# Moving one group of transposes into the second up unit, and the result stores to GpSimd's queue, in a graph-and-experts layer

## The chip, the cores and the metric

One core of a Trainium2 chip runs the whole layer. The metric is device time in microseconds (us). Three runs of the kernel before gave 1040.35, 1040.83 and 1041.01 us, median 1040.83.

## The reference, cut to what matters

A layer norm, two graph layers beside a linear attention, then a second layer norm and a mixture of experts over 625 rows of 1024 features. The change lies in the experts alone (8 routed experts, each row goes to 2; D = F = 1024):

```python
h = jax.nn.silu(jnp.einsum('nd,edf->nef', xf, w1))
ye = jnp.einsum('nef,efd->ned', h, w2)
routed = jnp.einsum('ne,ned->nd', combine, ye)
shared = jax.nn.sigmoid(xf @ shared_gate_w) * (jax.nn.silu(gate) * up @ shared_down)
return (routed + shared).reshape(b, t, d)
```

## The kernel before, in words

Every float32 product is made of three passes over a high and a low part of each operand (`passes`, L1985 to L1990). ScalarE (ACT) casts the high part, VectorE (DVE) subtracts it to get the low part. Weights stream from HBM in jobs of half a matrix, each in four pieces of 512 KB; `split_hi` (L789) and `split_lo` (L1186) split a piece, on ACT and DVE.

The expert stage works in blocks: seven fixed ones (q = 0 to 6, `expert`), each with rows of one expert, then a loop over dynamic blocks, which runs once on these inputs. Block q has one row tile or two (`ROWS_OF`, L55). Here q = 1 and q = 6 have one tile of 128 rows (`ONE`, L161); q = 0, 2, 3, 4, 5 have two and are "turned" (`TURNED`, L162): their second product comes out by features and is transposed back (`rows_back`, L2406); the loop's block has two and is not turned.

In a one-tile block TensorE (PE) computes the two up units ("hu", q, 0) and ("hu", q, 1), each 8 x 3 matmuls over half of the 1024 hidden features (`hidden_tokens`, L2422). ACT puts their silu into he_t (L1107). PE transposes each half of he_t with four 128 x 128 transposes (`hidden_across`, L2433, through `transposes`, L2030 to L2035). ACT casts the result (he high, L1117, through L805), DVE subtracts (he low, L1862, through L1205), and the down units ("y", q, h, s) read both (L2508). PE's order in such a block is: first up unit, the last transposes of the turned block before it (`rest_of`), second up unit, transposes of he_t's first half, 8 transposes of the next block's first rows (xg, `rows_across`), transposes of he_t's second half, down units. PE waits for he low by `arrivals` (L2459): first half before k = 0 of the first down unit, second half before k = 4.

Results go from PSUM to one of two staging rows y_s by ACT (`out_rows`, L1074). ACT waits for an earlier store of that row (`y_stored`), copies (L1083), frees the PSUM slot, and issues the store to expert_rows in HBM from its own queue (L1091).

GpSimd (POOL) fetches the next block's rows: `gather_rows(q + 1)` (L738; one indirect DMA for each row tile) as soon as DVE has done the low parts of block q's rows (`rows_in[q]`), so that xg is free. For the dynamic blocks `gather_block` (L746) first copies two index columns, drains, then issues two indirect DMAs. PE waits for them (`xg_loaded`, L2500). After the loop POOL waits for all stores (L772), then gathers each token's two expert rows (L777); DVE adds them up (L1938) and SP and ACT store the output.

PSUM is a ring of four slots in an order written out by hand (`units`, `between`, L168). Queues are in order. The DMA queues in the profile: q1 is SP's, q10 ACT's, q0 POOL's.

Of the kernel before, what the change touches and what calls it, by code (L numbers as in the profile page):

```python
# [5 lines left out]
def gps_layer(nc, x, src, dst, w_self0, w_neigh0, b0, w_self1, w_neigh1, b1,  # L6
# [31 lines left out]
    HW = D // 2  # L38
    HK = KF // 2
# [9 lines left out]
    BC = len(BROWS)  # L49
    CAPS = (208, 208, 152, 152, 152, 128, 128)  # L50
    ORDER = (3, 7, 1, 4, 2, 5, 6)
    FIXED = len(ORDER)
    assert sorted(ORDER) == list(range(1, X)) and len(CAPS) == FIXED and max(CAPS) <= B
    CAP = [CAPS[r - 1] for r in ORDER]
    ROWS_OF = [(128, c - 128) if c > 128 else (c,) for c in CAP] + [BROWS]  # L55
# [128 lines left out]
    LOOP = FIXED  # L184
# [55 lines left out]
    with ctx:  # L240
# [270 lines left out]
        lo_out = sem("lo_out")  # L511
# [156 lines left out]
        def _(pool):  # L668
# [69 lines left out]
            def gather_rows(q):  # L738

                for s, rows in enumerate(ROWS_OF[q]):  # L740
                    t = TILE_AT[q] + s
                    nc.gpsimd.indirect_dma_start(
                        out=xg[0:rows, s, :], out_offset=None, in_=xn2_d,
                        in_offset=bass.IndirectOffsetOnAxis(ap=cols_f[0:rows, t:t + 1], axis=0)).then_inc(xg_loaded, 16)

            def gather_block(at_block):  # L746

                for s in range(BC):
                    nc.gpsimd.tensor_copy(idx2[0:BROWS[s], s:s + 1], cols[0:BROWS[s], s, at_block])
                nc.gpsimd.drain()  # L750
                for s in range(BC):
                    nc.gpsimd.indirect_dma_start(
                        out=xg[0:BROWS[s], s, :], out_offset=None, in_=xn2_d,
                        in_offset=bass.IndirectOffsetOnAxis(ap=idx2[0:BROWS[s], s:s + 1], axis=0)).then_inc(xg_loaded, 16)

            gather_rows(0)
            for q in range(1, FIXED):
                pool.wait_ge(lo_out, rows_in[q - 1])
                gather_rows(q)
            pool.wait_ge(table_ready, 1)  # L760
            blocks = pool.value_load(table[0:1, 1, 0:1], min_val=1, max_val=MAXB - 1)
            pool.wait_ge(lo_out, rows_in[FIXED - 1])
            gather_block(slice(0, 1))
            with pool.Fori(0, blocks) as j:

                pool.wait_ge(lo_out, j * BR + R0)
                gather_block(bass.ds(j + 1, 1))

            pool.wait_ge(xg_loaded, blocks * (16 * BC) + gathered[LOOP])
            pool.wait_ge(lo_out, blocks * BR + R0)  # L770
# [12 lines left out]
        def _(act):  # L783
            copy = nc.scalar.copy

            def wait_unit(key, base=None):
                act.wait_ge(ready[slot(key)], use(key) + 1 if base is None else base * BU + (use(key) + 1))

            def split_hi(job, base=None, quarters=(0, 1), pieces=range(PARTS)):  # L789

                b = job % 2
                if job >= 2:
                    wait_unit(last_unit[job - 2], base)
                if job >= J_X:
                    for s in pieces:
                        act.wait_ge(part_loaded[(job - J_X) % 2][s], by(16 * ((job - J_X) // 2 + 1), base, 32))
                        copy(w_hi[b][:, s * PK:(s + 1) * PK, :], raw_part(job, s)).then_inc(hi_done, 1)  # L797
                    return
                for s in quarters:
                    act.wait_ge(w_loaded[s], 16 * (job + 1))  # L800
                    copy(w_hi[b][:, s * HK:(s + 1) * HK, :], w_raw[s][:, :, :]).then_inc(hi_done, 1)  # L801
# [272 lines left out]
            def out_rows(q, h, s, j=None):  # L1074

                key, tiles, rows = ("y", q, h, s), len(ROWS_OF[q]), ROWS_OF[q][s]
                wait_unit(key, j)

                b = row_buffer(q, h, s)
                before = stores[q][b] + (0 if ONE[q] else 16 * h)  # L1080
                if before:
                    act.wait_ge(y_stored[b], by(before, j, 32))
                copy(y_s[0:rows, b, :], PS(key)[0:rows, 0, :]).then_inc(y_copied, 1)  # L1083
                act.wait_ge(y_copied, by(copies[q] + h * tiles + s + 1, j, 2 * BC))
                act.sem_inc(free[slot(key)], 1)
                if j is None:
                    r = FIRST_ROW[q] + s * 128
                    to = y_d[r:r + rows, h * HW:(h + 1) * HW]
                else:
                    to = y_block(j, s, h * HW, (h + 1) * HW)  # L1090
                act.dma_start(to, y_s[0:rows, b, :]).then_inc(y_stored[b], 16)  # L1091

            def rest_of(q):

# [4 lines left out]
            def hidden_tokens(q):  # L1099

                job, rows = J_X + 4 * q, ROWS_OF[q][0]
                for h in range(2):
                    key = ("hu", q, h)
                    if h == 0:
                        split_hi(job + 1)
                    wait_unit(key)
                    nc.scalar.activation(he_t[0:rows, h, :], PS(key)[0:rows, 0, :], ACT.Silu).then_inc(silu_done, 1)  # L1107
                    act.wait_ge(silu_done, silus[q] + h + 1)
                    act.sem_inc(free[slot(key)], 1)
                    if h == 0:  # L1110
                        split_hi(job + 2)
                        rest_of(q - 1)

            def hidden_across(q, h):

                key, rows = ("ht", q, h), ROWS_OF[q][0]
                hi_of(key, he_hi[:, h * HK:(h + 1) * HK, 0:rows], PB(key)[:, 0:HK * rows].rearrange("p (k t) -> p k t", t=rows))  # L1117
# [28 lines left out]
            def expert(q, j=None):  # L1146

                job = J_X + 4 * q
                if ONE[q]:
                    hidden_tokens(q)  # L1150
                    hidden_across(q, 0)
                else:
                    hidden_features(q, j)
                for key in xe_units(q + 1)[:2]:
                    rows_hi(key, j)
                if ONE[q]:
                    hidden_across(q, 1)
                if TURNED[q]:
                    turned_out(q)
                    return  # L1160
                for h in range(2):
                    split_hi(job + 3 + h, j, pieces=range(PARTS) if h or ONE[q] else range(1, PARTS))
                    for s, rows in enumerate(ROWS_OF[q]):
                        out_rows(q, h, s, j)
                        if h == s == 0:
                            for later in xe_units(q + 1)[2:]:
                                rows_hi(later, j)
# [807 lines left out]
        def _(pe):  # L1975
# [21 lines left out]
            def weights_in(job, k, base=None):  # L1997

                if k % PK == 0:
                    pe.wait_ge(lo_done, by(count_at(job, k // PK), base, 4 * PARTS))  # L2000
# [421 lines left out]
            def hidden_tokens(q):  # L2422

                job, rows = J_X + 4 * q, ROWS_OF[q][0]
                for h in range(2):
                    key = ("hu", q, h)
                    claim(key)
                    by_tokens(key, PS(key)[0:rows, 0, :], (xe_hi, xe_lo), job + h, slice(0, rows),
                              comes=lambda k: weights_in(job + h, k)).then_inc(ready[slot(key)], 1)
                    if h == 0:  # L2430
                        rest_of(q - 1)

# [58 lines left out]
            def expert(q, j=None):  # L2491

                job = J_X + 4 * q
                pe.wait_ge(lo_out, by(rows_in[q], j, BR))
                if ONE[q]:
                    hidden_tokens(q)
                    hidden_across(q, 0)
                else:
                    hidden_features(q, j)
                pe.wait_ge(xg_loaded, by(gathered[q + 1], j, 16 * BC))  # L2500
                for key in xe_units(q + 1)[:2]:
                    rows_across(key, j)
                if TURNED[q]:
                    turned_out(q)
                    return
                if ONE[q]:
                    hidden_across(q, 1)
                for h in range(2):  # L2508
                    for s, rows in enumerate(ROWS_OF[q]):
                        key = ("y", q, h, s)  # L2510
                        claim(key, j)
                        by_tokens(key, PS(key)[0:rows, 0, :], HE, job + 2 + h, slice(s * 128, s * 128 + rows),
                                  arrives=arrivals(q, j) if h == s == 0 else None,
                                  comes=(lambda k: weights_in(job + 2 + h, k, j)) if s == 0 else None).then_inc(ready[slot(key)], 1)
                        if h == s == 0:
                            for later in xe_units(q + 1)[2:]:
                                rows_across(later, j)
# [43 lines left out]
```

## Time and profile before

| what | value |
|---|---|
| median of three runs | 1040.83 us |
| the profiled execution's own time | 1040.68 us |
| its span, first to last instruction | 1038.9 us |
| PE busy in the span | 1022.6 us (98%) |
| DVE, ACT, POOL busy | 63%, 44%, 8% |
| granted TensorE clock, mean | 0.999 of full speed |
| chain that ended last, by engine | PE 86%, DVE 4%, ACT 4%, DMA 2% |
| DMA queues' share of 16 engines' span | q1 35.7%, q0 5.4%, q10 2.1% |

The span plus 1.8 us is the execution's time. Expert blocks fill the stretch from about 704 to 1007 us; after 1007 us come the gathers of the results and the last products. A row of a timeline has the start in us, the duration in us, engine, line, operation, output and inputs, and in brackets the engine's idle time before it with what ended it. In a chain of waits each row is start, duration, and what the end of the kernel waited for at that time.

### The profile page before, as it was taken

The page shows a single profiled execution, that of the slowest core. Times are in us where ns is not written, and L with a number is a line of the kernel's source. Part 1 is how long each engine was busy: PE and PEld are TensorE (multiplying, and loading weights), DVE is VectorE, ACT ScalarE, POOL GpSimd, SP SyncE. Part 2 cuts the span into 40 slices and gives each one's busy share as a digit, 9 for nine tenths or more (in the row PEclk, how much of TensorE's full clock was granted, in tenths as well). Part 3 has the DMA queues.
Part 4 walks back from the last instruction along what each step waited for, and adds up shares of the span by engine and source line. Part 5 has one row for each costly group of instructions (what it writes and reads, how often), then busy time and mean ns, then how long its engine had stood idle before and what let it go on. Part 6 is the DMA issues. An engine that isn't in the chain of part 4 may idle for free.

```text
span 1038.9 us, 16292 instructions
## 1 busy us (share of the span) xinstructions
PE 1022.6 (98%) x6224; PEld 914.7 (88%) x6224; DVE 658.4 (63%) x970; ACT 460.2 (44%) x731; POOL 79.2 (8%) x123
## 2 busy tenths in 40 slices
PE   7999999999999999999999999999999999999998
PEld 5889998787888899987878899998989999998977
DVE  6789968666655765234337365124878787787846
ACT  4423344557777622221122342212666575567630
POOL 6000010000000000000000007000101000010103
PEclk9999999999999999999999999999999999999999
DMA  9821112033212221262200524233789677688918
GB/s 354 313 82 51 73 41 82 7 113 125 82 61 82 82 81 35 106 222 81 81 1 1 180 83 110 87 117 139 253 303 353 236 264 266 229 269 301 343 39 298
DMA packets 76694, 156.44 MB, mean 151 GB/s; under 512 B 8489, under 2 KB 8987, under 8 KB 76618
## 3 DMA queue, kind: packets, MB, share of 16 engines
q1 hardware_dynamic: 65656, 127.30, 35.7%
q0 software_dynamic: 6416, 20.00, 5.4%
q10 hardware_dynamic: 4546, 8.10, 2.1%
q8 instruction: 49, 0.80, 0.3%
q14 instruction: 27, 0.22, 0.1%
HBM read 133.89 MB, written 21.49 MB: 150 GB/s over the span
## 4 chain that ended last, share of the span: by engine, by line
PE 86%; DVE 4%; ACT 4%; DMA 2%; DVEq 2%; issue 1%; POOL 1%; ACTq 0%; POOLq 0%; SPq 0%
PE ps L1988 19%; PE ps L1990 19%; PE ps L1989 19%; PE ps L2452 7%; PE ps L2477 6%; PE ps L2453 3%; PE ps L2478 2%; PE ps L2087 1%; PE ps L2319 1%; PE ps L2250 1%; PE ps L2320 1%; PE ps L2251 1%; PE ps L2101 1%; PE ps L2034 1%; DMA y_second<-expert_rows,slots 1%
## 5 line engine op out<-in xcount | busy, mean ns | idle before, releaser
L1199 DVE TENSOR_TENSOR w_lo<-w_raw,w_hi 128x2048 fp32r<-128x2048 f32 x41 | 93.1, 2288 | 38.8 <-ACT w_hi L801 36.7
L2452 PE MATMUL ps<-xe,w_hi 128*128 128x304 f32 (+2 forms) x384 | 107.3, 357 | 0.0
L1988 PE MATMUL ps<-w_hi,xt_hi 128*128 128x512 f32 (+1 forms) x240 | 96.0, 400 | 3.5 <-DVEq L1509 2.0
L801 ACT CAST w_hi<-w_raw 128x2048 fp32r<-128x2048 f32 x41 | 77.1, 1908 | 45.2 <-PE ps L2320 36.2
L2453 PE MATMUL ps<-xe,w_lo 128*128 128x152 f32 (+2 forms) x384 | 94.4, 246 | 0.0
L1990 PE MATMUL ps<-w_hi,xt_lo 128*128 128x512 f32 (+1 forms) x240 | 93.6, 390 | 0.0
L1989 PE MATMUL ps<-w_lo,xt_hi 128*128 128x512 f32 (+1 forms) x240 | 93.6, 390 | 0.0
L1193 DVE TENSOR_TENSOR w_lo<-w_raw,w_hi 128x1024 fp32r<-128x1024 f32 x68 | 79.8, 1221 | 13.7 <-ACT w_hi L797 11.7
L2477 PE MATMUL ps<-he,w_hi 128*128 128x304 f32 (+1 forms) x320 | 88.2, 355 | 0.0
L797 ACT CAST w_hi<-w_late 128x1024 fp32r<-128x1024 f32 x64 | 63.0, 1053 | 45.0 <-PE ps L1990 18.4
L1193 DVE TENSOR_TENSOR w_lo<-w_late,w_hi 128x1024 fp32r<-128x1024 f32 x64 | 75.2, 1221 | 7.5 <-ACT w_hi L797 4.8
L797 ACT CAST w_hi<-w_raw 128x1024 fp32r<-128x1024 f32 x68 | 66.9, 1051 | 28.2 <-PE ps L2478 18.8
L1988 PE MATMUL ps<-xt_hi,w_hi 128*128 128x314 f32 x256 | 79.4, 310 | 0.0
L1989 PE MATMUL ps<-t_lo,w_hi 128*128 128x314 f32 x256 | 78.8, 308 | 0.0
L1988 PE MATMUL ps<-t_hi,w_hi 128*128 128x314 f32 x256 | 78.8, 308 | 0.0
L1990 PE MATMUL ps<-xt_hi,w_lo 128*128 128x314 f32 x256 | 78.7, 307 | 0.0
L1990 PE MATMUL ps<-t_hi,w_lo 128*128 128x314 f32 x256 | 78.7, 307 | 0.0
L1989 PE MATMUL ps<-xt_lo,w_hi 128*128 128x314 f32 x256 | 78.6, 307 | 0.0
L2478 PE MATMUL ps<-he,w_lo 128*128 128x152 f32 (+1 forms) x320 | 77.6, 242 | 0.0
L2453 PEld LDWEIGHTS ps<-xe,w_lo 128*128 128x128 f32 x384 | 73.3, 191 | 0.1
L2452 PEld LDWEIGHTS ps<-xe,w_hi 128*128 128x128 f32 x384 | 72.1, 188 | 1.3
L915 ACT ACTIVATE src_oh<-iota_c,src_f 128x128 f16<-128x128 bf16 x196 | 62.3, 389 | 19.6 <-DVE o_s L1576 15.0
(371 smaller groups left out, 2355.0 us busy)
## 6 DMA issues: line engine op xcount, KB each, us to landing
w_raw<-in_L_ffn_w SPq DMA_DIRECT2D x64, 512.0 KB, 5.7
w_late<-in_L_ffn_w SPq DMA_DIRECT2D x64, 512.0 KB, 5.1
w_raw<-in_L_gnn_W_neigh SPq DMA_DIRECT2D x8, 1024.0 KB, 6.0
w_raw<-in_L_gnn_W_self SPq DMA_DIRECT2D x8, 1024.0 KB, 5.1
w_raw<-in_L_ffn_shared_gate_up SPq DMA_DIRECT2D x8, 1024.0 KB, 6.0
expert_rows<-ctx_s POOLq DMA_DIRECT2D x15, 512.0 KB, 13.4
w_raw<-in_L_mix_Wv SPq DMA_DIRECT2D x4, 1024.0 KB, 14.8
w_raw<-in_L_mix_Wk SPq DMA_DIRECT2D x4, 1024.0 KB, 5.7
```

What stands on the lines that cost most here:

```text
L797: copy(w_hi[b][:, s * PK:(s + 1) * PK, :], raw_part(job, s)).then_inc(hi_done, 1)
L801: copy(w_hi[b][:, s * HK:(s + 1) * HK, :], w_raw[s][:, :, :]).then_inc(hi_done, 1)
L915: nc.scalar.activation(src_oh[b][:, c, :], iota_c[:, 0:128, 0], ACT.Abs, bias=src_f[:, g * GC + c:g * GC + c + 1]).then_inc(src_abs, 1)
L1193: V_.tensor_tensor(w_lo[b][:, k, :], raw_part(job, s), as32(w_hi[b][:, k, :]), ALU.subtract).then_inc(lo_done, 1)
L1199: V_.tensor_tensor(w_lo[b][:, k, :], w_raw[s][:, :, :], as32(w_hi[b][:, k, :]), ALU.subtract).then_inc(lo_done, 1)
L1988: mat(out_ap, lh, rh, start=start, stop=False)
L1989: mat(out_ap, lh, rl, start=False, stop=False)
L1990: return mat(out_ap, ll, rh, start=False, stop=stop)
L2452: mat(PS(key)[:, a, 0:2 * width], wh[:, k, w_cols], xe[:, :, k, 0:width], start=k == 0, stop=False)
L2453: last = mat(PS(key)[:, a, 0:width], wl[:, k, w_cols], xe_hi[:, k, 0:width], start=False, stop=k == KF - 1)
L2477: mat(PS(key)[:, a, 0:2 * width], wh[:, k, w_cols], he[:, :, k, 0:width], start=k == 0, stop=False)
L2478: last = mat(PS(key)[:, a, 0:width], wl[:, k, w_cols], he_hi[:, k, 0:width], start=False, stop=k == KF - 1)
```

## The change

Two edits. (1) In one-tile blocks the transposes of he_t's first half are called inside the second up unit, before its k = 4 (half of its 24 matmuls are issued then); ACT casts their result before the second half's silu; PE's and ACT's calls after the unit go away. (2) The stores of result rows leave ACT's program and are issued by POOL, each behind a wait for its copy (y_copied). In POOL's order the stores of block q - 1's second half (if turned) and of block q's first half (both halves, if q is not turned) stand behind the gather of block q + 1's rows; in the loop the four stores stand behind the gather.

```diff
--- before.py
+++ after.py
@@ -753,18 +753,39 @@
                         out=xg[0:BROWS[s], s, :], out_offset=None, in_=xn2_d,
                         in_offset=bass.IndirectOffsetOnAxis(ap=idx2[0:BROWS[s], s:s + 1], axis=0)).then_inc(xg_loaded, 16)
 
+            def store_rows(q, h, s, j=None):
+
+                rows, b = ROWS_OF[q][s], row_buffer(q, h, s)
+                pool.wait_ge(y_copied, by(copies[q] + h * len(ROWS_OF[q]) + s + 1, j, 2 * BC))
+                if j is None:
+                    r = FIRST_ROW[q] + s * 128
+                    to = y_d[r:r + rows, h * HW:(h + 1) * HW]
+                else:
+                    to = y_block(j, s, h * HW, (h + 1) * HW)
+                pool.dma_start(to, y_s[0:rows, b, :]).then_inc(y_stored[b], 16)
+
             gather_rows(0)
-            for q in range(1, FIXED):
-                pool.wait_ge(lo_out, rows_in[q - 1])
-                gather_rows(q)
             pool.wait_ge(table_ready, 1)
             blocks = pool.value_load(table[0:1, 1, 0:1], min_val=1, max_val=MAXB - 1)
-            pool.wait_ge(lo_out, rows_in[FIXED - 1])
-            gather_block(slice(0, 1))
+            for q in range(FIXED):
+                pool.wait_ge(lo_out, rows_in[q])
+                if q + 1 < FIXED:
+                    gather_rows(q + 1)
+                else:
+                    gather_block(slice(0, 1))
+                if q and TURNED[q - 1]:
+                    store_rows(q - 1, 1, 0)
+                    store_rows(q - 1, 1, 1)
+                for h in range(1 if TURNED[q] else 2):
+                    for s in range(len(ROWS_OF[q])):
+                        store_rows(q, h, s)
             with pool.Fori(0, blocks) as j:
 
                 pool.wait_ge(lo_out, j * BR + R0)
                 gather_block(bass.ds(j + 1, 1))
+                for h in range(2):
+                    for s in range(BC):
+                        store_rows(LOOP, h, s, j)
 
             pool.wait_ge(xg_loaded, blocks * (16 * BC) + gathered[LOOP])
             pool.wait_ge(lo_out, blocks * BR + R0)
@@ -1083,12 +1104,6 @@
                 copy(y_s[0:rows, b, :], PS(key)[0:rows, 0, :]).then_inc(y_copied, 1)
                 act.wait_ge(y_copied, by(copies[q] + h * tiles + s + 1, j, 2 * BC))
                 act.sem_inc(free[slot(key)], 1)
-                if j is None:
-                    r = FIRST_ROW[q] + s * 128
-                    to = y_d[r:r + rows, h * HW:(h + 1) * HW]
-                else:
-                    to = y_block(j, s, h * HW, (h + 1) * HW)
-                act.dma_start(to, y_s[0:rows, b, :]).then_inc(y_stored[b], 16)
 
             def rest_of(q):
 
@@ -1103,6 +1118,8 @@
                     key = ("hu", q, h)
                     if h == 0:
                         split_hi(job + 1)
+                    else:
+                        hidden_across(q, 0)
                     wait_unit(key)
                     nc.scalar.activation(he_t[0:rows, h, :], PS(key)[0:rows, 0, :], ACT.Silu).then_inc(silu_done, 1)
                     act.wait_ge(silu_done, silus[q] + h + 1)
@@ -1148,7 +1165,6 @@
                 job = J_X + 4 * q
                 if ONE[q]:
                     hidden_tokens(q)
-                    hidden_across(q, 0)
                 else:
                     hidden_features(q, j)
                 for key in xe_units(q + 1)[:2]:
@@ -2422,11 +2438,18 @@
             def hidden_tokens(q):
 
                 job, rows = J_X + 4 * q, ROWS_OF[q][0]
+
+                def arrive(h, k):
+
+                    weights_in(job + h, k)
+                    if h == 1 and k == HK:
+                        hidden_across(q, 0)
+
                 for h in range(2):
                     key = ("hu", q, h)
                     claim(key)
                     by_tokens(key, PS(key)[0:rows, 0, :], (xe_hi, xe_lo), job + h, slice(0, rows),
-                              comes=lambda k: weights_in(job + h, k)).then_inc(ready[slot(key)], 1)
+                              comes=lambda k: arrive(h, k)).then_inc(ready[slot(key)], 1)
                     if h == 0:
                         rest_of(q - 1)
 
@@ -2494,7 +2517,6 @@
                 pe.wait_ge(lo_out, by(rows_in[q], j, BR))
                 if ONE[q]:
                     hidden_tokens(q)
-                    hidden_across(q, 0)
                 else:
                     hidden_features(q, j)
                 pe.wait_ge(xg_loaded, by(gathered[q + 1], j, 16 * BC))
```

## Rows read from the trace of the kernel before

**Rows 1.** PE's waits from 700 to 1039 us: total, times, longest.

```profile
PE ps L1988 <- DVEq L1207: 1.8, 3, 0.7
```

**Rows 2.** Timeline of PE, block 1, around he_t's transposes.

```profile
770.25 0.60 PE L2034 MATMUL ps<-ident,he_t 128*128 128x128 f32 x4
770.69 1.04 PE L2034 MATMUL ps<-ident,xg 128*128 128x128 f32 x8
771.61 0.63 PE L2034 MATMUL ps<-ident,he_t 128*128 128x128 f32 x4
772.95 0.50 PE L1988 MATMUL ps<-w_hi,he 128*128 128x512 f32 x1 [0.71 <-DVEq L1207]
```

**Rows 3.** Chain of waits, block 1, from 769 to 773 us.

```profile
769.78 0.59 ACT y_s L1083
...
770.82 0.61 ACT he_t L1107
...
772.15 0.70 DVE he L1205
```

**Rows 4.** Timeline of PE, block 6: the same wait.

```profile
951.47 0.50 PE L1988 MATMUL ps<-w_hi,he 128*128 128x512 f32 x1 [0.71 <-DVEq L1207]
```

**Rows 5.** Timeline of PE, block 1: first matmuls behind a group of transposes.

```profile
764.67 0.47 PE L1988 MATMUL ps<-w_hi,xe 128*128 128x512 f32 x1
764.99 0.39 PE L1989 MATMUL ps<-w_lo,xe 128*128 128x512 f32 x1
765.22 0.40 PE L1990 MATMUL ps<-w_hi,xe 128*128 128x512 f32 x1
```

**Rows 6.** Timeline of DVE, block 1: weights split, and he low's second half.

```profile
765.93 4.63 DVE L1193 TENSOR_TENSOR w_lo<-w_raw,w_hi 128x1024 fp32r<-128x1024 f32 x4 [1.66 <-ACT w_hi L797]
...
774.66 0.69 DVE L1205 TENSOR_TENSOR he<-ps,he 128x512 fp32r<-128x512 f32 x1
```

**Rows 7.** Lines L1091 and L731: DMA issues by ACT and POOL (ns), and L731's landing.

```profile
L1091 ACTq DMA_DIRECT2D expert_rows<-y_s x28: 314/339/396, 754.8 to 1007.8; - x28
...
L731 POOL DMA_DIRECT2D cols_f<-token_of_slot x12: 532/563/617, 641.4 to 647.4; - x12
...
DMA to landing us min/median/max: 1.8/2.2/5.5
```

**Rows 8.** Chain of waits at the end: the last store.

```profile
1007.80 2.10 DMA expert_rows<-y_s
```

**Rows 9.** The page's second part: GB/s moved by DMA in 40 slices of the span.

```profile
GB/s 354 313 82 51 73 41 82 7 113 125 82 61 82 82 81 35 106 222 81 81 1 1 180 83 110 87 117 139 253 303 353 236 264 266 229 269 301 343 39 298
```

**Rows 10.** Timelines of POOL and DVE: gathers beside weight splits, and without them.

```profile
745.15 3.50 DVE L1193 TENSOR_TENSOR w_lo<-w_late,w_hi 128x1024 fp32r<-128x1024 f32 x3
...
745.27 1.91 POOL L742 DMA_INDIRECT xg<-xn_rows,cols_f  x1 [38.72 <-DVE xe L1205]
...
815.22 0.91 POOL L742 DMA_INDIRECT xg<-xn_rows,cols_f  x1 [0.30 <-issue]
```

**Rows 11.** Timeline of POOL: the dynamic block's first gather; landings of its second.

```profile
923.59 1.34 POOL L749 COPY idx<-cols 128x1 uint32<-128x1 uint32 x2 [31.80 <-DVE xe L1205]
...
930.01 1.32 POOL L752 DMA_INDIRECT xg<-xn_rows,idx  x1 [0.30 <-issue]
...
DMA to landing us min/median/max: 9.1/9.5/9.9
```

**Rows 12.** Timelines of ACT, DVE and PE around block 6.

```profile
933.79 0.58 ACT L1083 COPY y_s<-ps 24x512 f32<-24x512 f32 x1 [0.54 <-ACT y_s L1083]
...
938.16 4.63 DVE L1193 TENSOR_TENSOR w_lo<-w_late,w_hi 128x1024 fp32r<-128x1024 f32 x4 [0.29 <-ACT w_hi L797]
...
949.20 1.04 PE L2034 MATMUL ps<-ident,xg 128*128 128x128 f32 x8
```

**Rows 13.** Timeline of ACT, block 6's last copy; chain of waits, xg transposed in the loop.

```profile
963.42 0.59 ACT L1083 COPY y_s<-ps 128x512 f32<-128x512 f32 x1 [0.44 <-PE ps L1990]
...
983.44 0.87 PE ps L2034 x8
```

## The prediction

> **What bounds the kernel now.** I read the busy shares first: PE is busy in nearly the whole span at full clock, so only time in which PE waits, work added to PE, or the tail behind PE's last result can move the end. Then PE's waits in the expert stretch: three in 340 us, 1.8 us in total, the longest 0.7 [rows 1]. Two of these three are the wait that the change aims at. In block 1 PE transposes he_t's first half, xg, and he_t's second half, and then the first down matmul stands still for 0.71 us until DVE has he low [rows 2]. The chain of waits says why it comes late: ACT copies the turned block's last tile at 769.78, issues its store, does the second silu at 770.82, only then casts the first half, and DVE's subtraction runs from 772.15 to 772.85 [rows 3]. The first half's silu is over when the second up unit begins at 764.67 [rows 5], so its transposes wait for nothing but their place in the order. Block 6 repeats block 1 178.52 us later, wait included [rows 4]. Last, the chain at the end: PE's last down unit, ACT's copy, the store (issued 1007.80, landed 2.10 later), then POOL's gathers and the sums over them [rows 8]. What is added between the last copy and the first gather adds to the time in full.
>
> **The change, part by part.**
>
> Transposes of the first half, PE. The same four transposes are issued, at k = 4 of the second up unit. Nothing is saved in PE work; they spread from 770.25 to 770.69, 0.44 us [rows 2], and the unit ends that much later. One more switch from transposes back to matmuls is added: the first matmul behind such a group takes 0.32 us to the next one, where an ordinary pair is 0.23 apart [rows 5], so 0.09 us. PE waits there for silu 0 (done 3 us before) and a PSUM slot that the same silu frees: no wait.
>
> ACT. In block 1 the second copy ends at 770.37; without the store's issue before it (0.34 [rows 7]) it ends at about 770.0. The cast of the first half (0.6) follows, to 770.75. The second up unit, whose last matmul runs until about 770.4 now (the transposes are issued from 770.25 on), ends at 770.41 + 0.44 + 0.09 = 770.94, so silu 1 starts then, not at 770.82, and ends at 771.57 instead of 771.43. ACT is not late for it.
>
> DVE. Its weight split ends at 770.56 [rows 6], so it takes he low's first half from 770.85 to 771.55: before PE wants it.
>
> PE after that. xg's transposes end as before plus 0.09, at 771.70; the second half's transposes want silu 1, 0.14 later than before; they start at about 771.76 instead of 771.61 and need 0.44. The first down matmul starts at 772.20 instead of 772.95: **0.75 us saved**. The next thing that could be late is the second half at k = 4. Before, DVE had it at 774.66 + 0.69 = 775.35 [rows 6], and PE came to it at 772.95 + 0.34 + 11 x 0.23 = 775.8. Now DVE no longer has 0.69 us of first-half work between silu 1 and this one, so it is ready at about 774.6; PE comes at 775.05. No wait, 0.4 us of margin. Two blocks: **1.5 us saved**. Bounds: nothing, if the gap only moves to silu 1; 0.9 each (from the end of the transposes' issue, 771.61 + 0.44 = 772.05, to 772.95).
>
> The 28 stores leave ACT. 28 x 0.34 = 9.5 us of ACT's queue [rows 7]. PE waits for ACT nowhere but in the chain above, so beyond it this is worth nothing; the cover is PE's own unbroken work.
>
> The 28 stores on POOL. An issue there takes 0.56 us, and small transfers land 2.2 us after it [rows 7]. Nobody waits for 27 of them closely: the copy that reuses a staging row comes over 6 us later. The last one is on the path. ACT's store landed 2.10 us after its issue [rows 8]. Upper bound: POOL's 2.2, plus 0.55 for moving 192 KB at the page's fastest slice, 354 GB/s [rows 9], plus 0.1 for POOL to wake up, so 2.85 and +0.75; the lower bound is 0, if the issue is hidden in the landing. I take **+0.5 us**, near the upper bound, since both the issue (0.56 against 0.34) and the wake-up point upwards. The Trainium skill (DMA: Bandwidth & Descriptors, Latency and other measured facts) gives a first byte after about 1 us on GpSimd's path and 0.6 on ScalarE's; an estimate from that page alone would be +0.4. No run here shows it yet.
>
> POOL's order: what is queued behind the new waits. Gathers now stand behind the stores of the block before. Block 1's (of block 2's rows) went off at 745.27 [rows 10]; now it waits for block 0's copies, in block 1's mirror of 933.79 + 0.58 [rows 12], 755.9: start about 756.6, second tile 1.3 to 2.2 later, landed 9.9 after that at worst [rows 11], 768.7, needed at 770.7 [rows 2]. Turned blocks have 20 us. Block 6 is the tight one: its gather_block started at 923.59 [rows 11]. Now it stands behind copies that end near 934.0 (one ACT issue earlier than 934.37) and two issues: start about 935.0. PE wants xg at 949.20 + 0.09 [rows 12]. From the first index copy to the second gather's issue it took 6.4 us before [rows 11], beside a weight split; now DVE has no split until 938.16 [rows 12], so I take 3 us, the second gather goes off at 938.0 and lands by 947.9: in time by 1.4 us. In the loop the gather stands behind block 6's last copy, 963.42 + 0.59 [rows 13]: start about 965, landed by 965 + 6.4 + 9.9 = 981.3 at worst, wanted at 983.44 less 1.5 [rows 13]: just in time.
>
> How POOL fares beside DVE shows in a pair: 1.91 us for a gather's issue beside a weight split, 0.91 without one [rows 10]. The Trainium skill (SBUF — State Buffer, SBUF: two separate sides) says that descriptors written by GpSimd wait while VectorE holds the port pair they share, and advises ScalarE's or SyncE's queue: it speaks against this change. The trace agrees by the pair. It would act on stores and gathers in the middle, which nobody awaits; at the last store DVE splits nothing. As a rival it stands below, priced by rows.
>
> **Sum.** -1.5 + 0.5 = -1.0 against the profiled execution's 1040.68, which lies 0.15 below the median; against the median 1040.83 I say **1039.8 us**. About 0.2%, or 2.1 us, is what a measurement of this kernel can tell from no change, so the forecast is "same".
>
> **Rivals.**
> - *Gathers a bit late.* Preparing block 6's takes the full 6.4 us: 935.0 + 6.4 + 9.9 = 951.3, a stall of 2.0 us before xg's transposes, 1041.8. For: landings of 9.1 to 9.9 beside weight traffic. Against: DVE's pause in splits. Chance 0.12, mostly within 0.2%.
> - *POOL shut out beside the splits: slower.* Place: block 6's index copies. If two stores take POOL over 4.1 us instead of 1.1 from 934.0, it meets DVE's split from 938.16 to 942.8. Then 938.2 + 6.4 + 9.9 = 954.5, a stall of 5.2, and 1039.8 + 5.2 = 1045.0; part of it, 1043. The point from which it decides is 938.16. This is the skill's rule at its worst. Chance 0.09.
> - *The gap does not close.* PE finds silu 1 or a slot missing and stands still as long: +0.5, 1041.3. Against: every term above has a row. Chance 0.04.
> - *More than the wait.* 0.9 saved in each block, the tail for nothing, and some stalls that missing records hide: 1038.5. For: ACT loses 9.5 us of issues. Against: rows 1. Chance 0.09.
> - The forecast: 0.66, of which 0.04 reaches below 1038.75, if the tail is free and the bounds are met.
>
> **How the numbers follow.** Faster 0.04 + 0.09 = 0.13. Slower 0.09 + 0.03 (the worse part of the first rival) = 0.12. Within 0.2%: 0.75. The range 1038.6 to 1042.3 holds the forecast, the late gathers and the gap that stays; it leaves out the slower rival and most of the faster one, 0.18 together.
>
> **What would show it.** PE's waits for he low in blocks 1 and 6 gone, or under 0.1 us; the first down matmul some 0.75 us earlier after its second up unit began; ACT casting he before silu 1. POOL's store issues at 0.5 to 0.6 us, up to 1 longer beside weight splits; the last store landing 2.5 to 2.8 us after the issue, and about 2.9 us from the last copy's end to POOL's wake-up instead of 2.3. Block 6's second gather issued by 938 and landed before 948. Wrong would be a wait of PE for xg in block 6 or in the loop, or a first down matmul that now waits for silu 1.

## The result, and the profile after

The changed kernel takes 1046.39 us (median of six, 1044.94 to 1046.68) against 1040.59 for the kernel before (six, 1040.04 to 1041.01): ratio 1.0056, 95% interval 1.0046 to 1.0066. It is slower by 5.8 us, where I had forecast 1039.8 and a range to 1042.3. Times are medians of fast runs, which leaves out one of changed_warm at 2040.52 us.

PE's waits from 700 us on (total, times, longest), which answer to [rows 1]:

```profile
PE ps L2050 <- DMA xg<-xn_rows,idx: 4.4, 1, 4.4
PE ps L2004 <- DVEq L1223: 0.4, 1, 0.4
```

The two waits of 0.7 us for he low are gone; the one of 0.4 us stood before too, as the third of the three in [rows 1]. In their place stands one of 4.4 us for xg, the rows that POOL gathers. PE's timeline in block 1 (answers to [rows 2]) and in block 6:

```profile
771.75 0.63 PE L2050 MATMUL ps<-ident,he_t 128*128 128x128 f32 x4
772.13 0.48 PE L2004 MATMUL ps<-w_hi,he 128*128 128x512 f32 x1
...
952.91 1.97 PE L2050 MATMUL ps<-ident,xg 128*128 128x128 f32 x8 [4.38 <-DMA xg<-xn_rows,idx]
```

Block 1 does what was forecast: the first down matmul starts at 772.13 instead of 772.95, and the second up unit began 0.05 later than before (764.72), so 0.87 us are saved. In block 6 PE stands still for 4.38 us. POOL's timeline there, which answers to [rows 11]:

```profile
932.69 0.56 POOL L765 DMA_DIRECT2D expert_rows<-y_s  x1 [22.59 <-ACT y_s L1104]
933.42 0.54 POOL L765 DMA_DIRECT2D expert_rows<-y_s  x1 [0.18 <-issue]
933.96 0.33 POOL L749 COPY idx<-cols 128x1 uint32<-128x1 uint32 x2
942.61 1.03 POOL L752 DMA_INDIRECT xg<-xn_rows,idx  x1 [8.32 <-issue]
943.95 1.68 POOL L752 DMA_INDIRECT xg<-xn_rows,idx  x1 [0.30 <-issue]
```

POOL comes to gather_block at 933.96, a little earlier than the 935.0 of the sum, and copies both index columns in 0.33 us. Then 8.3 us pass. What fills them is the drain of L750. Its rows (shortest, median, longest in ns; first and last start), of the changed kernel and then of the kernel before; the first drain is the longest in both:

```profile
L750 POOLq DRAIN  x2: 7174/7776/8379, 933.5 to 970.3; - x2
```

```profile
L750 POOLq DRAIN  x2: 2467/3462/4456, 923.6 to 960.4; - x2
```

The first drain ends at 933.5 + 8.38 = 941.9. DVE's weight split of that time ends there too (937.29 + 4.63 = 941.92), so this trace alone does not say whether the drain waits for the stores or for DVE:

```profile
937.29 4.63 DVE L1209 TENSOR_TENSOR w_lo<-w_late,w_hi 128x1024 fp32r<-128x1024 f32 x4 [0.29 <-ACT w_hi L818]
```

The stores themselves take longer to land than the 2.2 us that I took from [rows 7], which are index loads. Landings of the result stores, as far as the traces have them, in the kernel before (from ACT's queue) and in the changed one (from POOL's):

```profile
DMA to landing us min/median/max: 2.1/6.2/7.8
```

```profile
DMA to landing us min/median/max: 2.3/5.8/7.3
```

The store issued last ahead of the drain (933.42) landed 6.1 us later, at 939.5.

The second gather lands 8.9 us after 943.95, at 952.85; PE had been ready at 948.5. The wait has a second price. The changed kernel's windows: length, busy time of PE, PEld, DVE, ACT and POOL (with counts), granted clock, DMA share, GB/s:

```profile
950.00:952.00 2.00, 0.00 (x0) 0.00 (x0) 0.00 (x0) 0.00 (x0) 0.00 (x0) 1.00 1.05 295
952.00:954.00 2.00, 1.08 (x5) 1.09 (x6) 0.00 (x0) 0.00 (x0) 0.00 (x0) 0.53 1.04 379
...
956.00:958.00 2.00, 2.00 (x6) 1.61 (x5) 1.59 (x3) 2.00 (x3) 0.00 (x0) 0.50 0.25 95
958.00:960.00 2.00, 2.00 (x8) 1.53 (x7) 2.00 (x3) 2.00 (x3) 0.00 (x0) 0.76 0.02 9
960.00:962.00 2.00, 2.00 (x11) 1.65 (x10) 1.96 (x2) 0.14 (x1) 0.00 (x0) 1.00 0.78 281
```

After 4 us of standing still, PE is granted 0.50 of its clock, the lower level of 1.2 GHz, until some time between 958 and 960. Last, the chain at the end, which answers to [rows 8]:

```profile
1012.57 0.59 ACT y_s L1104
...
1013.28 0.50 issue
...
1013.80 2.35 DMA expert_rows<-y_s
...
1016.18 0.79 issue
1016.98 1.02 POOL y_first L798
```

and the same in the kernel before:

```profile
1006.99 0.59 ACT y_s L1083
...
1007.80 2.10 DMA expert_rows<-y_s
...
1010.71 0.94 POOL y_first L777
```

From the last copy's end to the first gather 3.82 us pass (1013.16 to 1016.98); before, 3.13 (1007.58 to 1010.71).

The ledger of the two profiled executions: 0.05 ahead of block 1; -0.87 in block 1; then up to the last copy's end +5.58 - 0.05 + 0.87 = +6.40, which is block 6; +0.69 at the tail; -0.17 behind the first gather (last DVE row 1042.14 instead of 1036.04). Together 6.10, the difference of the spans. In block 6, the 4.38 of the wait less the 0.87 of the closed gap leave 2.89 us, which is the stretch at the lower clock. The trace of gather_first (below), which has the same matmuls without the wait, bears this out: until the wait its matmuls run 0.09 us behind those of the changed kernel, from 959.4 on 7.2 us ahead of them, so the wait and the stretch cost 7.3 us together.

### The profile page after: what moved, and what is told of

It is laid out like the page before. It is cut to its first block, busy times and chain, and to the rows that moved or that the text cites. A ratio compares the mean times of both kernels' runs of the same rounds, so it can differ in the third digit from the quotient of the medians.

```text
span 1045.0 us, 16296 instructions
## 1 busy us (share of the span) xinstructions
PE 1025.2 (98%) x6224; PEld 917.0 (88%) x6224; DVE 658.2 (63%) x970; ACT 460.8 (44%) x731; POOL 89.6 (9%) x151
## 4 chain that ended last, share of the span: by engine, by line
PE 86%; DVE 4%; DMA 3%; ACT 3%; issue 2%; DVEq 2%; POOL 1%; POOLq 0%; ACTq 0%; SPq 0%
PE ps L2004 19%; PE ps L2005 19%; PE ps L2006 19%; PE ps L2475 7%; PE ps L2500 6%; PE ps L2476 3%; PE ps L2501 2%; PE ps L2050 1%; PE ps L2103 1%; PE ps L2335 1%; PE ps L2336 1%; PE ps L2266 1%; PE ps L2267 1%; PE ps L2117 1%; DMA y_second<-expert_rows,slots 1%
```

## The experiments

Theory A: a drain on POOL ends only when the DMAs that POOL itself issued ahead of it have landed, so the fresh stores in front of gather_block hold the gather. Theory B, from the prediction: DVE's weight splits shut POOL out. Theory C: the gather is merely late. Code is shown in part; `...` marks what is left out.

**transposes_only.** The first edit alone, on the kernel before; L1091 stays on ACT.

```diff
+                    else:
+                        hidden_across(q, 0)
                     wait_unit(key)
...
+                    if h == 1 and k == HK:
+                        hidden_across(q, 0)
```

> Only the first edit (he_t's first half transposed inside the second up unit); the stores stay on ACT. If the loss comes from the stores on POOL, as I hold, block 6's first gather is issued at about 928.7 as before, PE waits for xg nowhere, and the two waits of 0.7 us for he low are gone: 0.87 us less in each block, as block 1 shows in the changed kernel, 1.7 us in all, 1038.9 us. If the moved transposes themselves cost something in block 6 (rival), that block is slower here too and the time is above 1040.

1039.45 us against 1040.44, ratio 0.9988 (0.9979 to 0.9997; the bracket is a 95% interval, here and below). No wait for xg. But it saves 1.0, not 1.7. PE's and ACT's timelines in its block 1:

```profile
772.43 0.63 PE L2035 MATMUL ps<-ident,he_t 128*128 128x128 f32 x4 [0.33 <-ACTq L1111]
```

```profile
770.80 0.32 ACTq L1091 DMA_DIRECT2D expert_rows<-y_s  x1
771.16 0.59 ACT L805 CAST he<-ps 128x512 fp32r<-128x512 f32 x1 [0.46 <-ACT y_s L1083]
771.64 0.60 ACT L1109 ACTIVATE he_t<-ps 128x512 f32<-128x512 f32 x1
```

With the two store issues in ACT's queue, the cast of the first half ends late and silu 1 behind it; PE waits 0.33 us for it in each one-tile block. So the stores' departure is worth something to PE once the transposes have moved.

**late_gather_act_stores.** The changed kernel with POOL's waits for y_copied kept, the stores back on ACT.

```diff
                 pool.wait_ge(y_copied, by(copies[q] + h * len(ROWS_OF[q]) + s + 1, j, 2 * BC))
...
-                pool.dma_start(to, y_s[0:rows, b, :]).then_inc(y_stored[b], 16)
...
                 act.sem_inc(free[slot(key)], 1)
...
+                act.dma_start(to, y_s[0:rows, b, :]).then_inc(y_stored[b], 16)
```

> The changed kernel with every wait of POOL's store code kept, but the stores themselves issued by ACT as before. So POOL reaches gather_block as late as in the changed kernel (about 933.5) with no DMA of its own in flight. Theory A, the drain in gather_block ends only when POOL's own stores ahead of it have landed: the drain is under 1.5 us, the gathers go off at about 935 to 937, no wait for xg, 1038.9 us. Theory B, DVE's weight splits keep POOL's drain from ending until they are over (the rival of the prediction): the drain again ends at about 942, a wait for xg of some 4 us, 1046 us. Theory C, the gather is merely late in the order: a wait for xg of 1 to 2 us.

1040.20 us against 1040.44, ratio 0.9995 (0.9986 to 1.0004). PE's wait for xg, the timeline of POOL, and the drain's row:

```profile
PE ps L2050 <- DMA xg<-xn_rows,idx: 1.8, 1, 1.8
```

```profile
934.19 0.30 POOL L749 COPY idx<-cols 128x1 uint32<-128x1 uint32 x2 [33.76 <-ACT y_s L1098]
938.29 1.48 POOL L752 DMA_INDIRECT xg<-xn_rows,idx  x1 [3.80 <-issue]
```

```profile
L750 POOLq DRAIN  x2: 742/2052/3362, 934.2 to 965.1; - x2
```

Same place in the order, copies started within 0.3 us, no store of POOL's in flight: the drain takes 3.4 us instead of 8.4 and 0.7 instead of 7.2. Five to six microseconds of each come with the stores. A's "under 1.5 us" and its 1038.9 us were missed: 3.4 us stay, and with them a wait of 1.8, which is what C expected. So both are at work: the late gather with the drain's other 3 us makes a wait of 1.8, the stores make it 4.4. Behind the wait of 1.8 the granted clock stayed at 1.00.

**drain_probe.** The kernel before, with a drain ahead of and one behind each gather of blocks 1 to 6.

```diff
                 pool.wait_ge(lo_out, rows_in[q - 1])
+                nc.gpsimd.drain()
                 gather_rows(q)
+                nc.gpsimd.drain()
```

> The kernel before with two more drains around each of POOL's gathers of blocks 1 to 6, one ahead (nothing of POOL's in flight) and one behind (its gathers in flight). Theory A: the one ahead takes under 0.5 us, the one behind as long as the gathers need to land, 5 to 9 us. Theory B: both take as long as DVE's weight splits run beside them (up to 4.6 us in blocks 1 and 2), and both are short in block 3, where DVE has only reductions out of PSUM there. No gather becomes late, so the time stays within 0.5 us of 1040.6.

1040.77 us in one run. The rows of the two drains, and the landings of the two gathers issued in block 1's place (the second at 747.79):

```profile
L759 POOLq DRAIN  x6: 53/53/2264, 704.6 to 890.9; - x6
```

```profile
L761 POOLq DRAIN  x6: 5704/7226/11005, 707.4 to 891.4; - x6
```

```profile
DMA to landing us min/median/max: 6.8/8.1/9.5
```

With nothing in flight the drain takes 53 ns in five cases of six; behind gathers it takes 5.7 to 11.0 us. The longest began at 746.4 and so ended at 757.4; the second gather landed at 747.79 + 9.5 = 757.3. The other five, too, end within 0.1 us of the last landing: in block 3 815.0 + 5.9 = 820.9 against 816.05 + 4.8 = 820.8, while a split of DVE's runs on to 821.3. This is theory A by itself, and B, by which the drain lasts as long as the splits, does not fit.

**no_drain_first.** The changed kernel; ahead of the loop, a semaphore of the two copies instead of the drain.

```diff
-                nc.gpsimd.drain()
...
+                if first:
+                    pool.wait_ge(idx_ready, BC)
+                else:
+                    nc.gpsimd.drain()
```

> The changed kernel, where in the gather_block before the loop a wait on the two index copies' own semaphore takes the place of the drain; the stores stay on POOL. Theory A: the gathers go off about 1 us after the copies, near 935, PE doesn't wait for xg in block 6, 1039.5 us (1.7 saved, 0.5 lost at the tail). Theory B (POOL shut out by DVE): no split runs from 933 to 937, so it gives the same here; C: the gathers still stand behind the stores, landing near 946, no or a short wait.

1039.35 us against 1040.44, ratio 0.9992 (0.9983 to 1.0001). 7 us faster than the changed kernel by one drain. The eleven executions spread from 1038.58 to 1041.88, and the profiled one is the slowest of them, 2.5 us above the median. Its POOL timeline, and PE's wait:

```profile
934.26 0.32 POOL L749 COPY idx<-cols 128x1 uint32<-128x1 uint32 x2
934.86 1.03 POOL L757 DMA_INDIRECT xg<-xn_rows,idx  x1 [0.27 <-POOL idx L749]
...
963.37 0.32 POOL L749 COPY idx<-cols 128x1 uint32 x2
972.78 1.03 POOL L757 DMA_INDIRECT xg<-xn_rows,idx  x1 [9.09 <-issue]
```

```profile
PE ps L2055 <- DMA xg<-xn_rows,idx: 1.4, 1, 1.4
```

Block 6 has no wait. The wait of 1.4 us is in the loop (at 983.35), where the drain was left: it took 8.8 us behind a store issued at 962.84 that landed 6.6 us later, at 969.4. It ended at 972.1. Whether the faster executions have this wait no trace shows.

**gather_first.** The changed kernel, stores of a block behind the gather of the next but one.

```diff
-                if q and TURNED[q - 1]:
-                    store_rows(q - 1, 1, 0)
-                    store_rows(q - 1, 1, 1)
...
+                for h in range(2 if q else 0):
+                    for s in range(len(ROWS_OF[q - 1])):
+                        store_rows(q - 1, h, s)
+            for h in range(2):
+                store_rows(FIXED - 1, h, 0)
```

> The changed kernel with another order in POOL's program: a block's stores all stand behind the gather of the next but one block, so block 6's gather_block stands where it stood before and the drain in it has no fresh store ahead of it. Theory A (the drain waits for the stores in flight ahead of it): block 6's first gather goes off at about 928.7 again, no wait for xg there, and with 1.7 saved in the two blocks and 0.7 lost at the tail the time is 1039.4 us. If DVE's splits were the cause, the drain would be as long as before the change, 3 to 4.5 us, and the time the same; so this one tells the order's share, not A from B.

1039.34 us against 1040.44, ratio 0.9989 (0.9980 to 0.9998): the time is as expected, and there is no wait for xg. Its copies, its gather in block 6, and the drain's row:

```profile
922.82 1.34 POOL L749 COPY idx<-cols 128x1 uint32<-128x1 uint32 x2 [12.64 <-DVE xe L1220]
929.46 1.21 POOL L752 DMA_INDIRECT xg<-xn_rows,idx  x1 [5.30 <-issue]
```

```profile
L750 POOLq DRAIN  x2: 5935/6446/6956, 922.8 to 963.0; - x2
```

The gather is not where I expected it. POOL came 0.8 us earlier than in the kernel before, and the gather went off 0.7 us later: the first drain took 5.9 us instead of 4.5, though POOL's last store, issued at 909.64, had landed by 915.6. The stores cost the drain time even when they have landed.

**late_gather_warm** and **changed_warm.** late_gather_act_stores and the changed kernel, each with one more drain far ahead.

```diff
+            nc.gpsimd.drain()
             gather_rows(0)
```

> late_gather_act_stores with one more drain on POOL ahead of block 0's gather (near 656 us), where nobody waits. There the drain in gather_block took 3.4 us though no DMA of POOL's was in flight. If that is because it is the first drain for a long time (drain_probe's first took 2.3 us, the next five 53 ns), it is now under 0.5 us, the gathers go off near 935.3, and the wait for xg of 1.8 us goes: 1.7 us faster than late_gather_act_stores, 1038.7 us. If it is the number of POOL's DMAs since the last drain, it stays above 1 us and part of the wait stays.

> The changed kernel with the same early drain on POOL. The drain in block 6's gather_block ended at 941.9, 2.4 us behind the last store's landing (939.5). If the early drain takes those 2.4 us away, it ends at 939.6 or so, the gathers go off at 940.3, and PE's wait for xg falls from 4.4 to about 2 us: 1046.4 less 2.4 and less of the slow-clock stretch, 1041 to 1043.5 us. If the 2.4 us come from DVE's weight splits from 937.3 to 941.9, nothing changes: 1046.

late_gather_warm: 1039.44 us against 1040.44, ratio 0.9992 (0.9983 to 1.0001); changed_warm: 1045.52 (five executions, 1042.18 to 1046.74), ratio 1.0042 (1.0029 to 1.0055). The early drain of the first and its drain in gather_block, then the drain's row, DVE's split and PE's wait of the second:

```profile
L761 POOLq DRAIN  x1: 2099/2099/2099, 656.3 to 656.3; - x1
L750 POOLq DRAIN  x2: 712/1019/1326, 934.5 to 963.9; - x2
```

```profile
L750 POOLq DRAIN  x2: 6273/6948/7623, 933.9 to 969.9; - x2
```

```profile
937.73 4.63 DVE L1210 TENSOR_TENSOR w_lo<-w_late,w_hi 128x1024 fp32r<-128x1024 f32 x4 [0.29 <-ACT w_hi L819]
```

```profile
PE ps L2051 <- DMA xg<-xn_rows,idx: 3.6, 1, 3.6
```

Without stores in flight the early drain takes 3.4 us down to 1.3, and the wait for xg goes (PE's wait for silu 1 stays, twice 0.33). It is not "under 0.5", but "above 1 us", which I had expected if the number of POOL's DMAs since the last drain counts. With stores in flight the early drain takes 0.8 us off, not 2.4. The last store landed at 933.86 + 6.3 = 940.2 and the drain ended at 941.5, while DVE's split ran on to 942.4: so it doesn't wait for the split to end. Of changed_warm's five executions the fastest, 1042.18, has a mean granted clock of 0.999, the other four (1044.93 to 1046.74) 0.996 or 0.997. It is some 3 us faster, as if it had no stretch at the lower clock; its trace was not taken.

**stores_only.** The second edit alone.

```diff
-                              comes=lambda k: arrive(h, k))
+                              comes=lambda k: weights_in(job + h, k))
...
                     hidden_tokens(q)
+                    hidden_across(q, 0)
```

> The second edit alone: stores on POOL, he_t's transposes where they were before. If the two edits act side by side, block 6 again waits for xg: PE comes to xg 0.5 us earlier than in the changed kernel (no transposes inside the second up unit), so its wait is about 4.9 us, with a stretch at the lower clock behind it; block 1 keeps its wait for he low, shorter by the two issues that left ACT (0.7 less 0.7, near zero to 0.3 left), the tail costs 0.7. That gives 1046.4 + 0.2 to 1.2: 1047 us.

1046.07 us against 1041.34, ratio 1.0046 (1.0029 to 1.0063). PE's waits:

```profile
PE ps L2049 <- DMA xg<-xn_rows,idx: 4.0, 1, 4.0
PE ps L2003 <- DVEq L1222: 0.8, 2, 0.4
```

One of the 0.4 is block 1's wait for he low, where it was 0.71: taking the issues off ACT alone gives 0.3 in a one-tile block. The loss (4.7 us here, 5.8 with both edits, with intervals that overlap) is the second edit's. The wait for xg was 4.0, not 4.9: POOL too came 0.8 us later there (copies at 934.77).

**deferred_stores.** transposes_only, with the two issues put behind the cast of the second half.

```diff
-                    out_rows(q, 1, 0)
-                    out_rows(q, 1, 1)
+                    out_rows(q, 1, 0, store=not ONE[q + 1])
+                    out_rows(q, 1, 1, store=not ONE[q + 1])
...
                     hidden_across(q, 1)
+                    if TURNED[q - 1]:
+                        store_rows(q - 1, 1, 0)
+                        store_rows(q - 1, 1, 1)
```

> The moved transposes with ACT's stores (transposes_only), where in a one-tile block ACT issues the two stores of the turned block's second half only behind the cast of he_t's second half, instead of ahead of silu 1. If the 0.33 us that PE waits for silu 1 in each of the two blocks of transposes_only is the price of these two issues, it goes, and the time is 0.7 us under transposes_only and 1.7 us under before: 1038.7 us. Rival: the copies or the cast alone keep silu 1 late; then it equals transposes_only.

1038.58 us against 1040.44, ratio 0.9983 (0.9974 to 0.9993): 1.9 us under the kernel before, and 0.9 under the median of transposes_only, though single executions of these two overlap (1038.27 to 1039.58 here, 1038.67 to 1040.09 there). PE's only wait from 700 us on, and its first down matmul in block 6, which has no idle time before it:

```profile
PE ps L1999 <- DVEq L1218: 0.4, 1, 0.4
```

```profile
949.67 0.48 PE L1999 MATMUL ps<-w_hi,he 128*128 128x512 f32 x1
```

It is 0.76 us under gather_first, which has the same blocks without waits but its last store on POOL.

## Why the prediction was wrong, point by point

**The transposes: right.** 0.75 us a block were forecast, 0.87 measured in block 1; nothing waits for silu 1 or for the second half. The sum had PE wait for silu 1 until 771.76; measured, the second half's transposes start at 771.75 with no idle time before them. What I called worth nothing, the issues that leave ACT, is part of it: transposes_only saves 0.5 a block, and the rest needs the stores out of the way. The sum contained this (the second copy ending at 770.0) without saying that the two edits lean on each other.

**The tail: right in sign, a little small.** +0.5 forecast, +0.69 measured, inside the bounds of 0 and 0.75. The landing took 2.35 us from the row's start instead of 2.10; the rest is that this row starts 0.64 behind the copy's end instead of 0.22. The Trainium skill (DMA: Bandwidth & Descriptors, Latency and other measured facts) gives GpSimd's path 0.4 us more to the first byte; the trace agrees in direction and shows 0.69 in all.

**POOL's order: the step that failed.** It read: "From the first index copy to the second gather's issue it took 6.4 us before [rows 11], beside a weight split; now DVE has no split until 938.16 [rows 12], so I take 3 us, the second gather goes off at 938.0 and lands by 947.9: in time by 1.4 us." Measured: 10.0 us (933.96 to 943.95), landed 952.85. The 6.4 holds a drain of 4.5 us that had no DMA of POOL's in flight ahead of it, and the 3 was a guess from it that put the difference down to the weight split. The split's part was about 1 us, in the copies (1.34 us beside it, 0.33 without); without a split and without stores of POOL's the same stretch still took 5.9 us (934.19 to 940.08, late_gather_act_stores). The change puts two fresh stores ahead of the drain, and the drain waits until they have landed: 53 ns without and 5.7 to 11 us with DMAs in flight (drain_probe), 3.4 against 8.4 us at the same place in the order (late_gather_act_stores against the changed kernel). I counted what is queued behind the stores, and costed the waits and the issues, but not that an instruction behind them could wait for their landing. The bound of 6.4 was therefore no bound. And the landing itself was mis-sized: I took 2.2 us for small transfers from index loads at 641 us, while the result stores of the kernel before, in the trace that I had, landed after 6.2 us in the median.

**The slower rival** had place and size nearly right (block 6, a stall of 5.2, 1045.0) and the mechanism wrong; that its time came within 1.4 us is luck, since 2.9 us of the measured one are the lower clock, which it did not have. It needed POOL to come to the copies after 938.16; POOL came at 933.96. I gave it 0.09. The rule of the Trainium skill behind it (SBUF — State Buffer, SBUF: two separate sides: descriptor writing on GpSimd is locked out by VectorE) acted little on the stores: an issue took 0.53 to 0.61 us, and 0.58 beside a split of DVE's (947.17). **The late-gather rival** (2.0 us of stall, 0.12) is what late_gather_act_stores shows, with 1.8: there is a 3 us part of the drain that isn't the stores' landing.

**What was in no term:** the lower clock behind a long wait, 2.9 us of the 6.4 in block 6.

**The drain's other part.** With nothing of POOL's in flight the drain is short in some places and long in others. The traces say more about this than my experiments asked. The table counts the DMAs that POOL had issued since its drain before, and gives the time from the end of the index copies ahead of the drain (from the drain's start where there are none) to its end:

| DMAs since the last drain | us | where |
|---|---|---|
| 0 | 0.05 to 0.1 | drain_probe: five drains ahead of gathers, and the first in gather_block |
| 2 | 0.2 to 0.3 | second drain in gather_block: before, late_gather_act_stores |
| 12 | 1.1 | late_gather_warm |
| 25 | 2.1 | the early drain of late_gather_warm |
| 27 | 2.3 | drain_probe, the first drain ahead of a gather |
| 37 | 3.1 | before (at 924 us), late_gather_act_stores (at 934 us) |
| 55 | 4.6 | gather_first |

The row of drain_probe's gather_block, to be held against the 4.5 us of the kernel before (1.34 of each are the copies):

```profile
L750 POOLq DRAIN  x2: 1433/1950/2468, 923.9 to 960.7; - x2
```

That is 0.08 to 0.09 us for each DMA from 12 DMAs on, landed long ago or not, beside splits or not. With DMAs in flight, too, the drain ends the later behind the last landing the more there were: 0.1 us at most (1 or 2 DMAs, drain_probe), 0.3 (6, the changed kernel's second drain), 1.3 (32, changed_warm), 2.4 (57, changed), 2.7 (63, no_drain_first). So the stores cost the first drain twice. Behind its copies it takes 3.1 us with no store of POOL's, 4.6 with 18 that have landed, 7.6 with 20 of which the last two are in flight.

**Open.** No experiment varied this number by itself, so it is read from traces and not shown by a run made for it. What POOL does in that time, and why only some half of it falls behind the landing when DMAs are in flight, stays open.

## What to carry to other kernels

A drain on GpSimd was here a wait for whatever DMAs GpSimd had in flight; before a DMA is moved ahead of one on that queue, ask how long it takes to land, there and beside that traffic, not how long it takes to issue. Where only a small copy has to be complete, let that copy's own semaphore say so. If issues stand in the way of an engine whose result is awaited, try first to put them later on the same engine: here (deferred_stores) that gave 1.9 us and left the tail as it was.

## What the runs showed of the hardware that I had not expected

GpSimd's drain waits for the DMAs that GpSimd has issued: 53 ns with none in flight and none issued since the drain before, 5.7 to 11.0 us with gathers in flight, each ending within 0.1 us of the last landing. It also grew with the number of DMAs issued since the drain before, all of them landed: 1.1 us at 12, 3.1 at 37, 4.6 at 55. And PE's wait of 4.4 us was followed by some 6 us at 0.50 of the clock (so were the waits of 3.6 us in changed_warm and 4.0 in stores_only), the wait of 1.8 us by none, so that the long wait cost 7.3 us for 4.4.
